# A recommendation tower on one core: one, four, five and five of the 12500-row tables looked up in on-chip sums instead of none, three, four and four

## The reference

```python
e = stack([tbl_f[ids[:, f]] for f in range(39)], axis=1)     # 2048 x 39 x 64
s = sum(e, axis=-1)                                           # only the row SUMS are used
z = s[:, _ROW] * s[:, _COL]                                   # all 741 pairs of fields
h = concatenate([z, dense_ctx], axis=1)                       # 757 columns
h = maximum(h @ W_top1 + b_top1, 0.0)                         # 757 x 512
h = maximum(h @ W_top2 + b_top2, 0.0)                         # 512 x 256
y = h @ W_top3                                                # 256 x 1
```

## Time and profile before

| | |
|---|---|
| runs | 198.95, 198.97, 199.9 us (median 198.97) |
| profiled execution | 199.26 us, of which the span from first to last instruction is 197.5 us |
| TensorE clock granted, mean | 0.965 |
| busy: PE / DVE / ACT / POOL | 173.5 / 127.0 / 81.2 / 136.4 us |
| DMA | 40.64 MB |

### The profile page before, as it was taken

How to read it: one execution, slowest core, us unless ns; L and a number is a source line. 1 busy time by engine, 2 the same in 40 slices (tenths; PEclk the granted TensorE clock), 3 DMA queues, 4 the chain that set the end, 5 groups by cost and what they waited for, 6 DMA issues and landing times.

```text
span 197.5 us, 4456 instructions
## 1 busy us (share of the span) xinstructions
PE 173.5 (88%) x1735; PEld 112.3 (57%) x1735; DVE 127.0 (64%) x328; ACT 81.2 (41%) x145; POOL 136.4 (69%) x140
## 2 busy tenths in 40 slices
PE   0598998768998799999578999999989899999993
PEld 0133543222786377666445767687756468767682
DVE  1611864687924864865858988987768977645440
ACT  0579798789001913415202320641141334233323
POOL 6777777778777777777877777877777777771000
PEclk9999999965599999999999999999999999999999
DMA  5998799999516935999999999111951111111000
GB/s 196 415 333 225 248 339 406 389 393 392 185 27 197 406 128 161 404 341 330 211 354 394 388 390 361 51 23 37 242 97 22 27 27 32 23 24 13 0 3 0
DMA packets 14549, 40.64 MB, mean 206 GB/s; under 512 B 3184, under 2 KB 5632, under 8 KB 14400
## 3 DMA queue, kind: packets, MB, share of 16 engines
q1 hardware_dynamic: 9872, 35.60, 50.4%
q0 software_dynamic: 4224, 4.33, 9.6%
q10 hardware_dynamic: 432, 0.42, 0.8%
HBM read 40.07 MB, written 0.27 MB: 204 GB/s over the span
## 4 chain that ended last, share of the span: by engine, by line
POOL 53%; PE 23%; issue 16%; DMA 4%; DVE 1%; ACT 1%; DVEq 0%
POOL rows L395 35%; POOL rows L404 18%; PE ph L1137 4%; PE ph L1141 4%; PE ph L1138 4%; DMA rows<-tab,idc 3%; PE ph L1157 2%; PE ph L1161 2%; PE ph L1158 2%; DMA idc<-ids_cols 2%; PE s L1116 1%; PE g L1076 1%; PE g L1051 1%; PE ph L1169 1%; DVE picked L509 0%
## 5 line engine op out<-in xcount | busy, mean ns | idle before, releaser
L395 POOL DMA_INDIRECT rows<-tab,idc x84 | 85.4, 1017 | 26.7 <-issue 25.3
L404 POOL DMA_INDIRECT rows<-tab,idc x48 | 48.8, 1017 | 14.6 <-issue 14.6
L1137 PE MATMUL ph<-z_hi,w_hi 126*128 126x512 f32 (+1 forms) x96 | 42.8, 446 | 0.5 <-ACT z_hi L839 0.4
L1141 PE MATMUL ph<-z_lo,w_hi 126*128 126x512 f32 (+1 forms) x96 | 39.3, 409 | 1.2 <-DVE z_lo L565 1.2
L1138 PE MATMUL ph<-z_hi,w_lo 126*128 126x512 f32 (+1 forms) x96 | 38.9, 405 | 0.0
L488 DVE TENSOR_SCALAR hots<-hots,fc 125x2048 bf16<-125x2048 bf16 x28 | 21.2, 771 | 14.8 <-ACT hots L788 14.0
L509 DVE SCALAR_TENSOR_TENSOR picked<-slot_b,fc,g 128x512 bf16<-128x512 bf16 x28 | 20.2, 742 | 7.1 <-PE g L1051 6.8
L1137 PEld LDWEIGHTS ph<-z_hi,w_hi 126*128 126x128 f32 (+1 forms) x96 | 18.9, 197 | 7.0 <-issue 3.3
L1141 PEld LDWEIGHTS ph<-z_lo,w_hi 126*128 126x128 f32 (+1 forms) x96 | 18.7, 195 | 7.4 <-DVE z_lo L565 3.2
L839 ACT CAST z_hi<-z 126x512 fp32r<-126x512 f32 (+1 forms) x24 | 14.7, 622 | 18.4 <-DVE z L559 18.3
L559 DVE TENSOR_TENSOR z<-factors,s 126x512 f32<-126x512 f32 (+1 forms) x24 | 15.9, 683 | 9.5 <-PE s L1116 6.6
(11 more groups left out here) (83 smaller groups left out, 225.7 us busy)
## 6 DMA issues: line engine op xcount, KB each, us to landing
stage<-middle SPq DMA_DIRECT2D x12, 800.0 KB, 10.0
hots<-shelf_scratch SPq DMA_DIRECT2D x17, 512.0 KB, 14.2
stage<-middle SPq DMA_DIRECT2D x4, 750.0 KB
stage<-early SPq DMA_DIRECT2D x3, 768.0 KB, 6.2
rows<-tab,idc POOLq DMA_INDIRECT x132, 3.9
stage<-early SPq DMA_DIRECT2D x3, 640.0 KB, 6.8
slot_b<-slot_scratch SPq DMA_DIRECT2D x8, 224.0 KB, 8.1
stage<-early SPq DMA_DIRECT2D x3, 512.0 KB, 3.9
```

The costliest lines, as they stand in the source:

```text
L395: pool.indirect_dma_start(rows[:, n % ROW_RING, i, :], None, gathered[i], bass.IndirectOffsetOnAxis(ap=idc[:, n, i:i + 1], axis=0)).then_i ...
L404: pool.indirect_dma_start(rows[:, n % ROW_RING, i, :], None, gathered[i], bass.IndirectOffsetOnAxis(ap=idc[:, n, i:i + 1], axis=0)).then_i ...
L1137: pe.matmul(ph[m][:, :], hi, z_hi[0:n, zi, :], start=(k == 0), stop=False)
L1141: mm = pe.matmul(ph[m][:, :], hi, z_lo[0:n, zi, :], start=False, stop=(k == KCH - 1))
```

## The change

Constants: `SUMMED` becomes `(1, 4, 5, 5)`, so five middle tables are loaded and summed. Code for summing a middle table on VectorE (`row_sum`, `split_rows`) is added, but `ROW_SUMMED` is empty: all five go the way of `mid_sum`. POOL's gathers become 28 + 16 + 12 + 12 = 68 in `fetch_a`, 48 in `fetch_b`. Chunk 0 gets a `mid_hot`, four `mid_look` and four `mid_pick` calls, and one more spread and shelf copy each in chunks 0 and 1. The seven slot copies of chunk 0 go from ScalarE to VectorE. `aparts` is widened from 32 to 128 columns, so `turn_a` writes all 128 partitions. The five mid-table shelves of chunks 2 and 3 are loaded by two DMAs instead of one. SP issues `load_middle(1)` ahead of `load_shelves(1, 4..6)`, `load_middle(3)` ahead of `load_shelves(2, ..)`, and `load_middle(4)` behind `load_slots(2)`. The order of the calls is new on VectorE, ScalarE and TensorE.

```diff
-SUMMED = (0, 3, 4, 4)
+SUMMED = (1, 4, 5, 5)
 NMID = max(SUMMED)
+ROW_SUMMED = ()
+PAIR_SUMMED = tuple(m for m in range(NMID) if m not in ROW_SUMMED)
...
-        aparts = sb("aparts", [P, TILES, LANE], BF16)
+        aparts = sb("aparts", [P, TILES, P], BF16)
...
-                sp.dma_start(mid_hots[:, 0:SUMMED[c], :],
-                             shelf_dram[c:c + 1, NE:NE + SUMMED[c], :]
+                n = min(SUMMED[c], 4)
+                sp.dma_start(mid_hots[:, 0:n, :],
+                             shelf_dram[c:c + 1, NE:NE + n, :]
                              .rearrange("c f n -> c (f n)").partition_broadcast(P)).then_inc(mid_hots_in, 16)
+                if SUMMED[c] > 4:
+                    a = mid_row(c, 4)
+                    sp.dma_start(mid_hots[:, 4:SUMMED[c], :], ...
...
+            def slot_copy(c, g, bank):                     # on VectorE, chunk 0
+                dve.wait_ge(slot_spread, c * GROUPS + g + 1)
+                dve.tensor_copy(slot_b[:, g, :], bank[:, :]).then_inc(slot0_copied, 1)
...
 VectorE, the beginning of the new order:
+            mid_ids(), ids(), split_dense(), hot(0, 0), split_tables(0), sum_a(0, 0), hot(0, 1)
+            slot_copy(0, 0, G0), slot_copy(0, 1, G1), hot(0, 2), pick(0, 0, G0), pick(0, 1, G1), hot(0, 3)
+            split_tables(1), slot_copy(0, 2, G0), hot(0, 4), slot_copy(0, 3, G1), pick(0, 2, G0), sum_a(0, 1)
+            pick(0, 3, G1), split_tables(2), slot_copy(0, 4, G0), slot_copy(0, 5, G1), hot(0, 5), hot(0, 6)
+            mid_hot(0), pick(0, 4, G1), slot_copy(0, 6, G0), split_w1(0), pick(0, 5, G1), pick(0, 6, G0)
+            sum_a(0, 2), split_w1(1), ..., split_w2(), split_w1(4), split_w1(5), multiply(0, 0), ...
...
 ScalarE, from the last shelf copies of chunk 0 on:
             shelf_copy(0, 27, S1)
+            shelf_copy(0, 28, S0)
             round_w1(0)
 ...
+            round_w1(4), round_w1(5), round_w2()
+            slot_copy(1, 0, G1), slot_copy(1, 1, G0), early_copy(0, G1)
+            shelf_copy(1, 0, G0), shelf_copy(1, 1, G1), shelf_copy(1, 2, G0), factor(0, "FE")
+            shelf_copy(1, 3, G1), shelf_copy(1, 4, G0), z_high(0, 0)
+            shelf_copy(1, 5, G1), shelf_copy(1, 6, G0), z_high(0, 1), ...
...
 TensorE, around the first look and around the first L1:
+            table_sum(1, 1), spread(0, 12), spread(0, 13)
+            pe.wait_ge(slot0_copied, 1)
             look(0, 0, G0)
+            pe.wait_ge(slot0_copied, 2)
             look(0, 1, G1)
+            spread(0, 14), spread(0, 15), table_sum(1, 2), spread(0, 16), table_sum(1, 3)
...
+            sum_lanes(0, G1), spread(1, 0) ... spread(1, 8) with sel(0, "FE"), sel(0, 0), sel(0, 1), sel(0, 2)
             L1(0, 0, 0)
+            spread(1, 9), L1(0, 0, 1), mid_sum(0, 0..3), spread(1, 10), L1(0, 0, 2), spread(1, 11), L1(0, 0, 3)
+            mid_look(0, 0, 0, 1, G1), mid_look(0, 1, 0, 1, G0), L1(0, 1, 0), ...
```

More of the change, by code:

```diff
@@ L246, in mid_picks, with mid_loads @@
             return sum(SUMMED[:c]) * TILES + t * SUMMED[c] + a
+        def mid_loads(c):
+            return 16 * sum(1 + (SUMMED[x] > 4) for x in range(2, c + 1))
         def rows_a(c):
@@ L602, in _ @@
             split_w1(3)
[L603 to L610, removed]
             split_w2()
-            sum_a(0, 3)
             split_w1(4)
             split_w1(5)
+            multiply(0, 0)
+            hot(1, 0)
+            multiply(0, 1)
+            z_low(0, 0)
+            multiply(0, 2)
+            sum_a(0, 3)
+            z_low(0, 1)
+            hot(1, 1)
+            z_low(0, 2)
+            sum_b(0, 0)
+            split_mid(0, G0)
+            hot(1, 2)
+            mid_pick(0, 0, 0, 1, G1, 1)
+            mid_pick(0, 1, 0, 1, G0, 2)
+            dve.wait_ge(mid_picked_ready, 1)
+            mid_pick(0, 2, 0, 1, G1, 3)
+            sum_b(0, 1)
+            dve.wait_ge(mid_picked_ready, 2)
+            mid_pick(0, 3, 0, 1, G0, 4)
             split_a(0)
[L616 to L619, removed]
             sum_b(0, 2)
+            sum_b(0, 3)
+            split_b(0)
+            split_mid(1, G0)
             multiply(0, 3)
@@ L963, in _ @@
             late_b(1, G0)
+            early_copy(2, G1)
             z_high(1, 5)
+            factor(2, "FE")
             h1_high(1, 0)
@@ L968, in _ @@
             h1_high(1, 3)
-            early_copy(2, G1)
-            factor(2, "FE")
             z_high(2, 0)
@@ L1217, in _ @@
             spread(0, 13, S1)
-            table_sum(0, 3)
+            pe.wait_ge(slot0_copied, 1)
+            look(0, 0, G0)
+            pe.wait_ge(slot0_copied, 2)
+            look(0, 1, G1)
             pe.wait_ge(shelf_copied, 13)
@@ new lines, in _ @@
+            spread(1, 8, G0)
+            L1(0, 0, 0)
+            pe.wait_ge(shelf_copied, 37)
+            spread(1, 9, G1)
+            L1(0, 0, 1)
+            pe.wait_ge(shelf_copied, 38)
+            mid_sum(0, 0, G0)
+            mid_sum(0, 1, G0)
+            mid_sum(0, 2, G0)
+            mid_sum(0, 3, G0)
+            pe.wait_ge(shelf_copied, 39)
+            spread(1, 10, G1)
+            L1(0, 0, 2)
+            pe.wait_ge(mid_calc, 2)
+            spread(1, 11, G0)
+            L1(0, 0, 3)
@@ L1386, in _ @@
             pe.wait_ge(picked_ready, 12)
-            look(1, 6, G0)
-            L2(0, 2, 0)
-            L2(0, 2, 1)
+            mid_sum(3, 0, G0)
+            mid_sum(3, 1, G0)
+            pe.wait_ge(picked_ready, 13)
+            look(1, 6, G1)
+            mid_sum(3, 2, G0)
+            mid_sum(3, 3, G0)
+            pe.wait_ge(picked_ready, 14)
+            sum_lanes(1, G1)
+            L2(0, 2, 1)
+            sel(1, "FE")
+            sel(1, 0)
+            pe.wait_ge(mid_calc, 14)
+            mid_look(1, 0, 0, 4, G0)
```

845 lines of the change are left out of this document (433 added, 412 removed).

## The result

The changed kernel takes 204.7 us (median of 203.32, 205.87, 203.53 and 206.08), against 198.96 for the kernel before in the same comparison: ratio 1.029, interval 1.019 to 1.040. It is slower, and its median lies beyond the end of the range (203.4), by 1.3 us. A second comparison gave 205.85 against 199.05, 1.026 (1.019 to 1.033).

What follows compares the result with a forecast made beforehand. PE was taken to bound the kernel, nearly full behind layer 1's start: 197.5 - 1.9 + 8.9 - 6.0 - 1.0 = 197.5 us span, so 199.0 against the median 198.97, no change; range from rival 1's 193.4 to rival 2's 203.4.

Steps and rivals of the forecast that it cites:

- start of layer 1: Head of the kernel: w1 issued near 23.0 instead of 28.18, layer 1 starting near 45.3, 1.9 us earlier.
- PE work behind: Behind layer 1's start: fifth table's sum, lookups, spreads and calls moved from ahead add 8.9 us of PE work.
- clock: Low granted clock, 3.7 us lost in layer 1 before: falls again, rises perhaps earlier, -1.0 us (bounds -3.7 and +4).
- PE idle behind: PE's 8.3 us of idle behind layer 1's start shrinks by 6.0 us; bounds on the idle left 0.5 and 8.
- I leave 2.3 us of idle: Behind layer 1's start: of PE's 8.3 us of idle, said to contain waits for POOL's late sums, 2.3 remain.
- the prediction's own signs of being wrong: POOL in chain after 100; PE idle above 5 us; VectorE gaps over 2; clock 1.00 over 30-55 or 0.5 before 38.
- the picks ahead of PE by a few tenths: Chunks 1 and 2 in the new order: VectorE's picks are ready a few tenths of a us before PE wants them.
- the likeliest case: Whole kernel: the even swap, no change at 199.0 us, own range 196.5 to 201.5, chance 0.50.
- The fifth table's load: SP's 3.15 MB more: costs 0, up to 2 us if it meets chunk 2's shelf loads.
- POOL: 16 fewer gathers save POOL 21 us; it leaves the path from chunk 1 on, and PE cannot take the gain.
- the 7 to 11: Bounds in us on PE's added work; outside them the prediction falls.
- rival 2: VectorE's queue sets the head, if copies exceed 0.7 us or first gather lands after 17: layer 1 at 49.7, 203.4 us; chance 0.18.

Runs made afterwards that it cites:

- the version with all three edits: Changed kernel with load_slots(3) ahead of load_mid_shelves(3), load_middle(4) behind load_shelves(2, 4..6), and sum_a(0, 0) behind pick(0, 1): 200.8 us.

## Why the prediction was wrong

By its own sum (start of layer 1, PE's work behind, PE's idle behind), for the profiled execution, forecast and measured:

```
                            forecast   measured
start of layer 1              -1.9       +0.1
PE work behind                +8.9       +6.3 }
clock                         -1.0       -2.0 } together +4.3
PE idle behind                -6.0       -0.3
span                           0.0       +4.0
```

(The measured start is where the stretches were cut, 47.30 for 47.20; the first product itself stands at 47.14 for 47.21. The terms add to +4.1; the last 0.1 lies behind the stretch. Only the +4.3 is measured: its division is an estimate. Before, 7.4 us of the low clock lay in layer 1 and cost 3.7; now 3.4 us of it lie behind the start and cost 1.7.)

**The failed step is "I leave 2.3 us of idle".** Measured: 8.0, inside the bound of 8 that I had written down, and at its far end. It is 5.7 us off, more than the whole miss: the start of layer 1 adds 2.0, and PE's work and the clock, 3.6 below the forecast, hide the rest. Three of the prediction's own signs of being wrong came with it: PE idle above 5 us, VectorE waiting over 2 us in the head (3.18), and the low clock ahead of 38 (36.9).

The first half of the step is where I took the idle time from. I wrote that the 8.3 us contained waits for POOL's late sums. VectorE did wait for gathered rows in the kernel before, 14.1 us behind the start of layer 1:

```profile
DVE bsum L532 <- DMA rows<-tab,idc: 10.8, 8, 2.6
DVE asum L527 <- DMA rows<-tab,idc: 3.3, 4, 1.0
```

But of PE's waits there the largest two end with the split of a middle table (2.3) and z_lo (1.2), and only one piece of the latter, 0.5 us at 147.31, follows directly on such a wait. How much of the rest came from POOL by longer ways is not shown; no row bore a relief of 6.0.

The second half is what the new order adds. I walked VectorE's and PE's queues and found "the picks ahead of PE by a few tenths"; I did not walk SP's queue past `load_mid_shelves(3)`, whose wait for `mid_look(2, 3)` I could read in the code. The new order moves `pick(3, 0)` nearer to that lookup, and `load_slots(3)` behind it has a landing of 7.7 us that nothing covers any more. With the slots first the time is 1.9% less, 201.0, inside the likeliest case's own range (196.5 to 201.5). That is not the sum come true: in its profiled execution (198.46) PE is still idle 6.8 us behind the start of layer 1, 4.5 more than forecast, and busy 139.9, 5.4 less than forecast.

**The fifth table's load "fits: 0, and up to 2 us if it meets the shelf loads of chunk 2".** It meets them: 2.1 us at the place named. The bound was right and the value chosen wrong. DMA's mean share of 0.57 says nothing of this; over 109.00 to 116.00 it is 1.03. And the wait brings a second cost that the sum had no term for (the clock, below).

**POOL: right that it leaves the path, and that PE cannot take the 21 us.** POOL's last gather starts at 156.55 (157 said), and no POOL piece is in the chain behind 100. Put back into the new order, the gathers cost 6.5 us (4.8 to 8.3), about the 6.0 that I took for the relief. The agreement is partly luck: the 6.0 stood for PE's idle behind the start of layer 1 alone, and the 6.5 has a part in the head and one in the clock. In the old order the relief was not measured on an ordinary chip.

**PE's added work: over, by the products moved.** From the groups of instructions of the changed kernel (busy us, mean ns), and last the sums of the version with the slots first:

```profile
L1087 PE MATMUL g<-stage,fc 128*32 128x100 f32 x630 | 17.6, 267 | 1.0 <-issue 1.0
...
L1133 PE MATMUL g<-mparts,mid_hots 125*128 125x100 bf16 x180 | 9.9, 208 | 3.6 <-DVE picked L553 2.5 <-DVE mid_picked L562 1.1
...
L1141 PE MATMUL g<-bc,aparts 128*128 128x128 bf16 x16 | 1.6, 222 | 0.0
...
L1087 PE MATMUL g<-stage,fc 128*32 128x100 f32 x630 | 16.1, 250 | 1.5 <-issue 1.5
```

The sums went from 13.4 to 17.6. At 2.4 GHz throughout they take 16.1, +2.7 (3.4 said); the other 1.5 is the low clock. The lookups went from 7.5 to 9.9, +2.4 (2.5 said); `turn_a` with its wider weights stayed at 1.6 (0 said). What is left of the 6.3 is 1.2, for the products moved behind the start of layer 1 and one more spread (3.0 said). With 6.3 the work lies below the 7 to 11 outside which the prediction was to fall, and PE's busy time is 174.0, not near 180.

**The clock gave more than said at one place and took some back at another.** The granted clock ahead of the first fall, in it, behind the start of layer 1, and where PE waits for the shelves:

```profile
33.40:36.90 3.50, 1.39 (x14) 0.36 (x13) 3.50 (x7) 2.75 (x7) 2.59 (x4) 0.99 1.03 391
36.90:43.70 6.80, 5.32 (x19) 1.37 (x20) 6.47 (x10) 5.56 (x11) 5.89 (x4) 0.50 1.01 386
47.30:54.60 7.30, 7.30 (x150) 5.54 (x149) 4.87 (x12) 3.24 (x7) 5.77 (x6) 1.00 0.59 195
109.00:116.00 7.00, 4.94 (x127) 4.51 (x120) 4.84 (x8) 1.01 (x2) 5.17 (x7) 0.76 1.03 382
```

Before, the clock was 0.51 over 40.80 to 54.60 and 7.4 us of that lay in layer 1. Now the fall comes some 4 us earlier, at 36.9, behind a stretch in which PE was busy 1.39 of 3.50, and lasts half as long, so that the clock is back at 2.4 GHz when layer 1 starts. The 3.7 us are regained, where I took 1.0. But it falls to 1.2 GHz once more around 112, behind the 2.1 us wait for the shelves, for 3.4 us, and all of that lies in the fifth table's sum. Groups of 94 instructions of a table's sum in the changed kernel, at the upper clock and there:

```profile
63.39 2.26 PE L1087 MATMUL g<-stage,fc 128*32 128x100 f32 x94
...
111.86 3.90 PE L1087 MATMUL g<-stage,fc 128*32 128x100 f32 x94
```

So the wait for the shelves cost twice, 2.1 and another 1.6. In the profiled execution with the slots first PE waits 1.7 at this place, is busy 5.77 of 7.00, and the clock stays at 1.00:

```profile
109.00:116.00 7.00, 5.77 (x118) 4.55 (x118) 6.64 (x14) 0.62 (x1) 5.47 (x6) 1.00 1.02 382
```

That is no effect of the edit, which lies behind this stretch. The Trainium skill, "TensorE: Matmul & The Clock Gate", section "What's actually happening", has the throttled state as the default that activity releases. Both falls, each behind a stretch in which PE waited, agree with that; why the first one ended so much sooner than before is not shown.

**Start of layer 1: 1.8 us late.** VectorE in the head:

```profile
18.81 0.62 DVE L571 TENSOR_REDUCE asum<-rows 128x7 f32<-128x448 f32 x1 [3.18 <-DMA rows<-tab,idc]
19.35 0.74 DVE L526 TENSOR_SCALAR hots<-hots,fc 125x2048 bf16<-125x2048 bf16 x1
20.01 1.28 DVE L539 CAST slot_b<-g 128x512 bf16<-128x512 f32 x2
```

The gather issued at 12.37 took 6.42 us to land, not the 4.6 of one row, and came at 18.8, not 16.3. w1 was issued at 25.83 (23.0 said) and layer 1 started at 47.14 (45.3 said). This is rival 2's condition (later than 17) without its price: it asked for 49.7. That the late gather is the cause is not shown: with the sum moved out of its way (the version with all three edits) w1 went out earlier and layer 1 did not start earlier. The profiled executions of the same head start at 45.47, 47.14, 48.68 and 48.81, so no forecast of it is better than some 1.5 us. The copies out of PSUM stand 0.60 apart, as chosen, each 0.68 long. The Trainium skill, "VectorE: DVE Perf Modes", section on the TRN2 errata, gives 120 + FD/Accel cycles at 0.96 GHz for such a copy, an estimate of 0.66 unaccelerated: the row agrees, and the accelerated 0.39 is ruled out.

The two waits for loads have one root: I walked the engines' queues, and of the queue that issues the loads I asked where a call moved, not what stands in front of it and how long it lands. The two other misses, the idle time credited to POOL and the price of the moved products, had no row behind them that measured the thing itself.

## What to carry to other kernels

When calls are reordered so that a consumer comes earlier, walk the queue that issues its load up to the first wait in front of it, and add the landing; a load that is free to go must not stand behind one that waits for the previous chunk. Relief of an engine that runs tightly beside the bound is worth only what its lateness costs the bound engine, here 6.5 of 21 us in the new order. Before it is counted, follow the bound engine's own waits back to it. In the one stretch tried here with DMA's share near 1.0, moving one load past another only renamed the wait.

## What the runs showed of the hardware

On three of the chips the kernel before took 331 to 333 us instead of 199. There, in the changed kernel, from 20 to 40 us (busy of PE, weight loads, VectorE, ScalarE, POOL; clock; DMA share; GB/s):

```profile
20.00:40.00 20.00, 4.07 (x16) 1.65 (x14) 0.00 (x0) 0.00 (x0) 15.12 (x17) 0.50 0.14 27
```

POOL gathers at its usual pace, all other engines nearly stand, and nothing that the trace shows holds them. PE's largest entry is 51.6 us of "issue" in 50 pieces of up to 2.5. Sixteen gathers more or fewer are then worth 20 to 28 us, and the change is 3.4% faster there than before (0.967). That the engines' instructions come late while gathers are issued would fit; no run tested it.

On the ordinary chips a small indirect transfer of 32 KB landed between 3.1 and 5.9 us after issue in the median of the kernels, and a shelf load of 512 KB 11.2 to 14.2 (one load of a middle table's shelves in the changed kernel took 17.9); a load's landing is to be taken from the stretch in which it will run, not from the one figure of the profile's page.
